# A bidirectional selective scan with experts: the first unit's dt and du spread by TensorE, gathers and loads moved, chunks 2 and 3 reordered

## What is computed

```python
h = table[x, slice 3]                                   # [2, 2048, 64]
a = ln(h)
c, gate = split(LN(a) @ in_w.T)                         # 128 channels each
act = silu(dwconv4(c) + conv_b)
for d in ("f", "b"):                                    # b runs backwards in time
    xd, z = split(act @ d.in_w.T)
    xd = silu(dwconv4(xd) + d.conv_b)
    dt8, B, C = split(xd @ d.xproj_w.T)                 # 8, 16, 16
    dt = softplus(dt8 @ d.dt_w.T + d.dt_b)
    h_t = h_t-1 * exp(dt_t * A) + dt_t * xd_t * B_t     # 128 channels x 16 states
    y = sum_n h_t[n] * C_t[n] + xd * D
    m[d] = (y * silu(z)) @ d.out_w.T
h += concat(m) * silu(gate, gate) @ out_w.T + a
n = ln(h); e = argmax(n @ router_w.T + router_b)        # 1 of 32 experts
h += relu(relu(n @ W1[e] + b1[e]) @ W2[e] + b2[e])
```

## Time and profile before

| what | value |
|---|---|
| median of 3 runs | 554.76 us (552.57 to 560.9) |
| the profiled execution's own time | 554.74 us |
| its span (first to last instruction) | 552.9 us |
| mean granted TensorE clock | 0.935 of full |
| DVE (VectorE), POOL (GpSimd) busy | 87%, 86% of the span |
| PE (TensorE), ACT (ScalarE) busy | 84%, 68% |

### The profile page before, as it was taken

How to read it: one execution, slowest core, us unless ns; L and a number is a source line. 1 busy time by engine, 2 the same in 40 slices (tenths; PEclk the granted TensorE clock), 3 DMA queues, 4 the chain that set the end, 5 groups by cost and what they waited for, 6 DMA issues and landing times.

```text
span 552.9 us, 5695 instructions
## 1 busy us (share of the span) xinstructions
PE 463.2 (84%) x1653; PEld 180.2 (33%) x1653; DVE 481.8 (87%) x591; ACT 376.7 (68%) x666; POOL 474.9 (86%) x157
## 2 busy tenths in 40 slices
PE   2977968878799797979898889888988987795987
PEld 1422322323233332324233424342334332332343
DVE  2675985989898998999989989999999999999951
ACT  2488685686867786777858497869785885364643
POOL 5552799998989999899999998999999999999800
PEclk9999989999989897989799799999998997796999
DMA  4149795958392936648384839293949395830000
GB/s 58 16 61 213 157 200 124 209 143 178 95 206 70 199 97 155 155 113 181 100 168 138 182 114 195 85 207 103 198 112 202 98 196 123 188 60 9 0 11 19
DMA packets 51008, 71.05 MB, mean 129 GB/s; under 512 B 16498, under 2 KB 17442, under 8 KB 50978
## 3 DMA queue, kind: packets, MB, share of 16 engines
q1 hardware_dynamic: 47986, 69.36, 55.3%
q0 software_dynamic: 1024, 1.05, 2.7%
q10 hardware_dynamic: 1968, 0.29, 0.3%
HBM read 60.19 MB, written 10.49 MB: 128 GB/s over the span
## 4 chain that ended last, share of the span: by engine, by line
DVE 38%; PE 37%; issue 10%; ACT 7%; POOL 3%; DMA 2%; SPq 2%; DVEq 0%; ACTq 0%
DVE st L1529 21%; DVE st L1514 8%; PE ps L630 5%; PE ps L729 3%; PE ps L717 3%; PE ps L692 3%; PE ps L811 2%; POOL st L491 2%; PE ps L657 2%; PE ps L700 2%; PE ps L705 2%; ACT ps L1094 2%; PE ps L669 1%; PE ps L745 1%; DVE zr L1535 1%
## 5 line engine op out<-in xcount | busy, mean ns | idle before, releaser
L491 POOL TENSOR_TENSOR st<-st,repC 128x2048 f32<-128x2048 f32 x63 | 285.2, 4529 | 20.0 <-ACT carry L1100 14.4
L1529 DVE TENSOR_TENSOR_SCAN st<-ps,carry,st 128x512 f32<-128x512 f32 x192 | 235.1, 1267 | 4.7 <-ACT ps L1094 3.8
L1094 ACT ACTIVATE ps<-dtS,negA 128x512 f32<-128x512 f32 x256 | 170.8, 681 | 48.3 <-DVE st L1529 47.3
L482 POOL TENSOR_TENSOR st<-duS,repB 128x2048 f32<-128x2048 f32 x30 | 135.9, 4530 | 0.5 <-DMA duS<-du_dram 0.5
L1529 DVE TENSOR_TENSOR_SCAN st<-ps,zero,st 128x512 f32<-128x512 f32 x64 | 78.8, 1269 | 5.3 <-ACT ps L1094 4.9
L717 PE MATMUL ps<-st,fold 128*32 128x512 f32 x504 | 69.6, 625 | 12.8 <-POOL st L491 12.8
L1514 DVE TENSOR_TENSOR st<-duS,ps 128x2048 f32<-128x2048 f32 x33 | 74.9, 2270 | 0.2 <-issue 0.2
L630 PE MATMUL ps<-act,wT 128*128 128x512 f32 x128 | 57.8, 593 | 0.3 <-ACT act L1037 0.3
L463 POOL DMA_INDIRECT x<-in_L_tok_ple_table,idx x32 | 31.0, 968 | 29.4 <-DMA dtS<-dt_dram 13.0
L692 PE MATMUL ps<-xr,Bw 128*128 128x512 f32 x68 | 38.2, 645 | 7.9 <-ACT bc_sb L1086 6.2
L669 PE MATMUL ps<-xr,wT 128*32 128x512 f32 x32 | 20.4, 725 | 22.3 <-DVE st L1514 22.3
(11 more groups left out here) (141 smaller groups left out, 634.0 us busy)
## 6 DMA issues: line engine op xcount, KB each, us to landing
repC<-bc_dram SPq DMA_DIRECT2D x64, 256.0 KB, 10.4
duS<-du_dram SPq DMA_DIRECT2D x60, 256.0 KB, 4.4
dtS<-dt_dram SPq DMA_DIRECT2D x60, 256.0 KB, 7.4
repB<-bc_dram SPq DMA_DIRECT2D x60, 128.0 KB, 3.0
dt_dram<-dt SPq DMA_DIRECT2D x16, 256.0 KB, 3.2
du_dram<-du SPq DMA_DIRECT2D x16, 256.0 KB, 2.0
bc_dram<-bc_sb SPq DMA_DIRECT2D x16, 64.0 KB, 11.1
dtS<-dt_dram SPq DMA_DIRECT2D x8, 128.0 KB, 3.0
```

Of the source, the lines that this page charges most:

```text
L482: pool.tensor_tensor(st[:, r], duS[:, u % 2], row, ALU.mult).then_inc(sem("dbu_pool"), 1)
L491: pool.tensor_tensor(st[:, r], st[:, r], row, ALU.mult).then_inc(sem("hc_ready"), 1)
L1094: sc.activation(decay_bank(u, r, q), dtS[:, u % 2, q], ACT.Exp, scale=negA[:, way(u), q, r:r + 1]).then_inc(sem("decay_ready"), 1)
L1529: dve.tensor_tensor_scan(st[:, r, q, order], decay_bank(u, r, q)[:, order], st[:, r, q, order], first, ALU.mult, ALU.add).then_inc(sem("sc ...
```

## The change

1. Unit 0's first group does not wait for DRAM. A selection matrix `sel` (made by VectorE from the identity) lets TensorE spread dt and du by a product for each quarter (`spread_dt`, `spread_du`) into PSUM; ScalarE's `first_decay` and VectorE's `first_product` read them there, B's row standing as a copy in `ga`. Groups 1 to 3 still use `dtS` and `duS` from DRAM.
2. The first softplus: relu, plus one and the sums are VectorE's, abs, exp and Ln ScalarE's.
3. GpSimd issues its last 12 gathers in one row ahead of `by_c(0, 0)`, and `dt_times_x(1)` stands behind it. Before, 8 stood ahead and 4 behind `by_c(0, 2)`.
4. On ScalarE `softplus_in(1)` and `softplus_exp(1)` stand ahead of group 1's decays; `gate_silu(0)` is in the first burst of unit 0 and with it `keep_last(0, 1)`; `decay_rates(1)` stands behind decay 6; the first burst stands behind decay 8 (it was 6), the second behind decay 13 (it was 11).
5. On TensorE `x_chunk(2)` stands ahead of `sum_dt(1)`, `gate_chunk(0)` behind `x_chunk(3)`, and `conv(2)` behind `sum_states(0, 0)`. On VectorE steps of the norms of chunks 2 and 3 stand between other tiles.
6. SyncE issues the experts' loads in unit 3 instead of ahead of unit 0's loop.

```diff
@@ SyncE
             load_C(1)
-            with nc.allow_non_contiguous_dma(reason="b1 is 2 KB"):
-                for dst, src in late_loads:
-                    sp.dma_start(dst, src).then_inc(sem("late_in"), 16)
             for u in range(UNITS):
...
                     load_dt(u + 2)
+                if u == 3:
+                    with nc.allow_non_contiguous_dma(reason="b1 is 2 KB"):
+                        for dst, src in late_loads:
+                            sp.dma_start(dst, src).then_inc(sem("late_in"), 16)
@@ GpSimd
                 if u == 0:
-                    pool.wait_ge(sem("dt_first_1"), 64)
-                    for t in range(TB + 4, TB + 12):
+                    pool.wait_ge(sem("du_in_dram"), 16)
+                    for t in range(TB + 4, TILES):
                         gather(t)
-                    dt_times_x(1)
...
                 by_c(u, 0)
+                if u == 0:
+                    pool.wait_ge(sem("du_spread"), NQ)
+                    dt_times_x(1)
                 by_c(u, 1)
@@ TensorE
+            def spread_dt(q):
+
+                pe.wait_ge(sem("dt_ready"), 1)
+                if q == 0:
+                    pe.wait_ge(sem("sel_ready"), 1)
+                    pe.wait_ge(sem("dtproj_ready"), 2)
+                if q == NQ - 1:
+                    pe.wait_ge(sem("scanned"), 1)
+                pe.matmul(ps[:, q % 3, :], sel[:, q], dt[:], start=True, stop=True).then_inc(sem("dt_spread"), 1)
+
+            def spread_du(q):
+
+                pe.wait_ge(sem("du_ready"), 1)
+                if q >= 2:
+                    pe.wait_ge(sem("dbu_first"), q - 1)
+                elif q:
+                    pe.wait_ge(sem("b_first"), 1)
+                else:
+                    pe.wait_ge(sem("wT_late"), 1)
+                pe.matmul(ps[:, SHORT if q % 2 else Y, :], sel[:, q], du[:], start=True, stop=True).then_inc(sem("du_spread"), 1)
+
@@ ScalarE
             exp_ln_tables()
+            sc.wait_ge(sem("pre_ps"), 1)
+            sc.activation(e_[:], ps[:, PRE, :], ACT.Abs, bias=dt_b[:, 0:1]).then_inc(sem("abs_first"), 1)
+            sc.wait_ge(sem("abs_first"), 1)
+            sc.activation(e_[:], e_[:], ACT.Exp, scale=-1.0).then_inc(sem("sp_e"), 1)
+            sc.wait_ge(sem("sp_w"), 1)
+            sc.activation(l_[:], dt[:], ACT.Ln).then_inc(sem("sp_l"), 1)
+            bc_out(0)
             squares(2)
             rsqrt(1)
-            softplus_in(0)
-            softplus_exp(0)
-            softplus_plus1(0)
-            softplus_ln(0)
+            sc.wait_ge(sem("b_ps"), 1)
+            sc.activation(ga[:], ps[:, SHORT, :], ACT.Copy).then_inc(sem("b_first"), 1)
+            sc.wait_ge(sem("rates_ready"), 1)
+
+            def first_decay(q):
+
+                sc.wait_ge(sem("dt_spread"), q + 1)
+                sc.activation(decay_bank(0, 0, q), ps[:, q % 3, :], ACT.Exp, scale=negA[:, 0, q, 0:1]) \
+                  .then_inc(sem("decay_ready"), 1)
+
+            first_decay(0)
+            first_decay(1)
+            uT_chunk(1)
...
+            first_decay(2)
+            first_decay(3)
             silu_tables()
-            gate_silu(0, 0)
-            act_silu(1, 1)
+            act_silu(1, PRE)
...
+            keep_last(0, 0)
+            softplus_in(1)
+            bc_out(1)
+            softplus_exp(1)
@@ VectorE
+                dve.wait_ge(sem("sp_e"), 1)
+                dve.tensor_scalar(dt[:], e_[:], 1.0, None, ALU.add).then_inc(sem("sp_w"), 1)
...
+            def first_product(q):
+
+                dve.wait_ge(sem("du_spread"), q + 1)
...
+                dve.tensor_tensor(st[:, 0, q], ps[:, SHORT if q % 2 else Y, :], ga[:], ALU.mult).then_inc(sem(done[0]), 1)
```

More of the change, by code:

```diff
@@ L849, in _ @@
             write_nought(2, 0)
+            b_rows(0, 0)
+            spread_dt(0)
+            spread_du(0)
+            spread_dt(1)
+            spread_du(1)
             turn_chunk(1)
-            gate_chunk(0, 0)
-            b_rows(0, 0)
-            x_chunk(1, 1)
+            spread_dt(2)
+            spread_dt(3)
+            spread_du(2)
+            x_chunk(1, PRE)
             turn_chunk(2)
-            conv(1, 2)
+            spread_du(3)
+            conv(1, PRE)
+            b_rows(0, 1)
             pre(1)
@@ L858, in _ @@
             skip_product(0)
-            add_nought(3)
+            add_nought(1)
             turn_chunk(3)
-            b_rows(0, 1)
+            b_rows(0, 2)
+            x_chunk(2, LONG)
             sum_dt(1)
-            x_chunk(2, LONG)
-            b_rows(0, 2)
             x_chunk(3, ZED)
-            conv(2, PRE)
+            gate_chunk(0, PRE)
             b_rows(0, 3)
             sum_states(0, 0)
+            conv(2, PRE)
             zed(0, ZED, 0)
@@ L1088, in decay @@
             def decay(u, r, q):
-                if u == 0 and r == 0:
+                if u == 0 and r == 1:
                     sc.wait_ge(sem(f"dt_first_{q // 2}"), 64)
-                elif r == 0 and q == 0:
+                elif u and r == 0 and q == 0:
                     sc.wait_ge(sem(f"dtS_in_{u % 2}"), spread(u))
@@ L1323, in first_unit @@
                     bc_out(2)
-            for p in range(NR * NQ):
+            for p in range(NQ, NR * NQ):
                 decay(0, p // NQ, p % NQ)
@@ L1485, in _ @@
             begin_norm(1)
-            norm_var(1)
-            begin_norm(2)
             ch.mark(dve.tensor_scalar(minus[:], ident[:], -1.0, None, ALU.mult))
-            ch.mark(dve.memset(xfT[DM:XR], 1.0))
             ch.mark(dve.memset(w1[XR - 1:XR], 0.0))
             ch.mark(dve.memset(router_wT[DM:DM + E, :], 0.0))
+            dve.wait_ge(sem("consts"), 1)
+            ch.mark(dve.tensor_copy(rank[:], ranki[:]))
+            ch.mark(dve.tensor_copy(w1[DM:DM + E], maskf))
+            norm_var(1)
+            ch.mark(dve.memset(xfT[DM:XR], 1.0))
+            begin_norm(2)
+            dve.wait_ge(sem("abs_first"), 1)
+            dve.tensor_scalar(v_[:], ps[:, PRE, :], dt_b[:, 0:1], 0.0, ALU.add, ALU.max).then_inc(sem("sp_a"), 2)
+            dve.wait_ge(sem("sp_a"), 2)
+            first_softplus()
             norm_newton(1)
@@ L1658, in between @@
                         finish(u - 2)
[L1660 to L1665 removed]
+            def first_product(q):
+                dve.wait_ge(sem("du_spread"), q + 1)
+                if q == 0:
+                    dve.wait_ge(sem("b_first"), 1)
                     dve.wait_ge(sem("dtproj_ready"), 2)
                     dve.wait_ge(sem("wT_copied"), 9)
[L1668 to L1670 removed]
+                done = ("dbu_first", q + 1) if q < NQ - 1 else ("dbu_dve", 1)
+                dve.tensor_tensor(st[:, 0, q], ps[:, SHORT if q % 2 else Y, :], ga[:], ALU.mult).then_inc(sem(done[0]), 1)
+                dve.wait_ge(sem(done[0]), done[1])
             def first_unit(p):
                 if p == 0:
+                    norm_newton(2)
+                    start_u2(2)
+                if p == 1:
+                    start_residual(2)
+                    begin_norm(3)
+                if p == 3:
+                    norm_var(3)
                     norm_newton(3)
                     start_u2(3)
[L1677 removed]
+                    input_product(0, 1)
+                if p == 4:
                     log1p_error(1)
                     start_residual(3)
[L1680 to L1682 removed]
+                if p == 6:
                     input_product(0, 2)
[L1684 removed]
+                if p == 7:
+                    rates(1)
+                if p == 9:
                     input_product(0, 3)
```

88 lines of the change are left out of this document (32 added, 56 removed).

## The result

The changed kernel took 565.32 us (median of four runs, 560.85 to 572.21) and the kernel before 555.89 us (median of four, 552.57 to 560.9). Measured a second time, in twelve runs, the changed kernel took 559.93 us against 555.15, ratio 1.0088 (1.0039 to 1.0136). That median is inside the range, and the two intervals overlap; why the medians differ is a good part of the question. The three profiled later took 562.09, 560.18 and 569.0 us.

A forecast was written before the change was run, and what follows sets the result against it. VectorE and GpSimd were taken to set the units' pace, so only the head could change: -9.4 at the first product, +4.4 until group 1's product, +6.7 in the bursts, 1.7 on 554.74, giving 556.4 us; range 549.5 to 561.

The forecast's parts named there:

- the milestone: Error term of unit 3's softplus on VectorE, at 91.96 us before: moves the end one for one; forecast 93.7.
- First dt and du, first scans: Start of unit 0: dt and du 2.6 us earlier, VectorE's first product 9.4 us earlier, at 38.75.
- The lead shrinks: Unit 0 up to group 1's product: lead falls from 9.4 to 5.0 us; dt_out(1) comes 3.4 us late.
- bursts: ScalarE's two bursts of silus in unit 0 and the order around them: cost 6.7 us; VectorE waits 3.3 and 3.5.
- G: The 12 gathers moved into GpSimd's idle hole in unit 0; forecast as hidden.
- Gathers into GpSimd's hole: 12 gathers, 15 us from 40.1, fill GpSimd's wait in unit 0; worth nothing on the path.
- rival of 2.6 us through repC alone: Gathers delay repC(0), so by_c(0, 0) and conv(2) behind its sum come late: 2.6 us, 559.0; chance 0.08.
- O: The new order of the engines' work in unit 0; priced at 1.7 us later.
- Experts' loads: SyncE's loads in unit 3: 11.5 us covered by 43, no effect; rival that they hit the path, 567.9, chance 0.03.
- Lead survives: Rival: VectorE keeps the 5.0 us it has at group 1's product, 549.7 us; chance 0.23.
- no early scans: Rival: the spreads wait as long as the copies did, scans start at 48, over 565 us; chance 0.02.
- the clock: Rival: TensorE falls to half clock in the gap before x_chunk(2), 3.5 us on the path, 559.9; chance 0.08.

The follow-up runs named there:

- e8: Changed kernel with gathers as before, plus a TensorE product of zeros on each side of b_rows(0, 2): 556.42 us, ratio 1.0.
- Experiment 1: Changed kernel with the gathers put back as before (8 early, 4 behind by_c(0, 2)): 558.86 us, ratio 1.0045.
- experiment 9: Products of zeros before b_rows(1, 1): six in the kernel before, ratio 0.9985; four in the changed kernel with old gathers and sum_dt(1) first, 1.0028.
- experiment 3: Changed kernel with its 12 gathers held until the first copies of dt and du have landed: 562.33 us, ratio 1.0125.
- experiment 5: Changed kernel with both the gathers and the experts' loads put back as before: 559.49 us, ratio 1.0087.
- experiment 2: Kernel before with only the gathers moved, all 12 in one row behind du_in_dram: 557.74 us, ratio 1.0055.

## Why the prediction was wrong

*What bounds the kernel, and the milestone:* right as the place where the change acts: 16.3 of the 17.5 us of the first profile lie ahead of it. "One for one" is not shown. Behind the error term the profiles took 457.8 to 464.4 us, and e8, with 2.6 us more head than before, has a ratio of 1.0.

*First dt and du, first scans:* right. du ended at 35.47 (35.75), first product at 38.43 (38.75). 2.9 and 9.7 us were won (2.6 and 9.4), and worth nothing at the end, as argued.

*The lead shrinks; bursts; bc_out(2):* the mechanism right, the term too small. This is the step whose failure the experiments show best. Experiment 1 has this order without G, and with its start put on that of before (+0.5) its steps are: product of group 1 53.1 (53.2), uT_chunk(3) 56.2 (56.5), dt_out(1) 64.1 (62.65), scan 9 69.9 (68.4) with a wait of 4.82 (3.3), second burst from 75.3 (73.75), wait before scan 14 3.56 (3.5), bc_out(2) 83.8 (82.40), error term 95.0 (93.7). All is within 0.4 up to uT_chunk(3), and from dt_out(1) on 1.3 to 1.6 late. The term mis-sized is "1.71 + 3 x 0.86 = 4.3" ahead of dt_out(1): from x_chunk(2) to the end of its sum it measured 6.1 (57.36 to 63.42). I left out TensorE's half clock behind its new gap, on the strength of one row (1.12 us after 1.65 idle). The same program point took 1.92 in experiment 9. One row had shown one of two outcomes. The Trainium skill's statement (TensorE: Matmul & The Clock Gate, Part 1) that the low level is the default pointed the right way. This made 3.0 us of 1.7. (In the first burst my terms, 1.28 + 2.1 + 1.28, add up to 4.66, where I wrote 4.5; it took 4.45.)

*Gathers into GpSimd's hole, "hidden":* this step failed as well. I reckoned GpSimd's time and its queue, and it is true that GpSimd had the hole. I treated the DMA engines, at 0.99 in the earlier trace rows, as a doubtful rival of 2.6 us through repC alone. The runs showed that 12 gathers among the copies lower what the engines move (146 to 212 GB/s instead of 229), stretch SyncE's issues (repC's four took up to 8.18 us) and delay duS and repC. That cost 3.5 us of head in one execution (562.09 us, which the ratios leave out) and nothing in two others. In the old order the move goes with 0.55% of the time. In the new order on one chip it is 0.4 us in the medians, not to be told from nothing. The rival's conv(2) mechanism was seen by itself in experiment 3.

*What put the first measurement outside the range* is shown only in part. O and the gathers' 0 to 3.5 us, put on the 554.74 of before, give 557.8 to 561.3; the second measurement, 559.93, lies between. In the two longest profiles (572.21 and 569.0 us) the 8 us for which ScalarE stands still with its input in place are most of what the head has beyond that of experiment 1. What causes that wait is open, and so is whether the executions between, at 564 to 567 us, had it.

*Experts' loads:* right, nothing (1.0007).

*Lead survives, no early scans:* neither happened.

*The size in the medians:* the head's 3.0 us are 0.5% of the whole. Experiment 1 measures 0.45%, but experiment 5, which has the same order and head, 0.87%, so the agreement of the first is in part luck. The second measurement of the changed kernel, 1.0088, stands against my 1.003; of these 0.6%, some 3 us, the mis-sized term makes 1.3, and the rest is not attributed, since experiment 5 has the same 1.0087 without the early gathers. The range's upper end took the clock or the gathers, not both, and no stall at all.

## What to carry to other kernels

An engine's idle hole is free only if what is put there uses nothing else that is busy in it: before moving DMA issues, look at the DMA share of that stretch, and at 0.99 count the move as a possible cost. Where one execution shows a short product after an idle TensorE, take both levels into the range, and count every gap that an order opens ahead of a product on the path. When a profile shows a loss beside an edit, look whether it begins before the edited instruction runs: in experiment 2 it did. And read a loss relative to an event in the program, since the landing of the first loads shifts whole traces by more than the effects sought.

## What the runs showed of the hardware

- A gather's packet of about 1 KB took 0.10 us (experiment 1, 54 to 56 us), 0.26 to 0.30 or 0.42 us beside copies, whose packets took 0.10 to 0.13. In the dearest case gathers had half of the engines' time for a seventh of the bytes.
- ScalarE stood still for about 8 us with its input in place, twice in sixteen profiles, both times with gathers and copies together on the DMA engines and in a profile that names few releasers. Four profiles with the 12 gathers in one row in the new order, on another chip, don't have it.
- The same wait at the same place of TensorE was followed by full clock in one execution and by half clock in another (1.65 us idle: 1.12 and 1.92; 1.34 and 1.35 us idle: 1.99 and 3.78 for a pair), or by half clock sooner or later (4.23 us idle: 1.31 and 2.04), so one profile doesn't give a gap's price.
- The clock of a whole execution varied with it: the kernel before took 560.1 to 560.4 us in runs with a mean granted clock of 0.926 and 552.9 at 0.954, in one series, which is as much as the whole effect of the change (not without exception: 552.5 at 0.938).
